# Attention and a routed expert layer on one core: most normalisers of the linear attention sent through memory instead of through TensorE, and turned tokens and logits in one product

## What is computed

```python
q, k, v = jnp.split(x @ W_qkv, 3, axis=-1)          # 16 heads of 64
q, k = relu(q @ W_f + b_f), relu(k @ W_f + b_f)
kv = einsum('bhnd,bhne->bhde', k, v)
out = einsum('bhnd,bhde->bhne', q, kv)
normalizer = einsum('bhnd,bhd->bhn', q, k.sum(axis=2))
out = out / (normalizer[..., None] + 1e-06)
x = layernorm(x + out @ W_out + b_out)
probs = softmax(x @ gate_w.T); topk_probs, topk_idx = top_k(probs, 2)
y = for each of the two: gelu(x @ w1[e] + b1[e]) @ w2[e] + b2[e]
x = layernorm(x + sum(y * topk_probs))
```

## Time and profile before

| | us |
|---|---|
| median of three runs | 456.76 |
| lowest and highest | 455.43, 457.03 |
| profiled execution | 455.49 |
| its span from first to last instruction | 453.7 |
| PE busy | 426.3 |
| DVE busy | 323.0 |
| ACT busy | 276.7 |
| POOL busy | 162.5 |
| mean granted TensorE clock | 0.983 of full speed |

### The profile page before, as it was taken

One profiled execution on the slowest core, in us unless ns is written; L12 is line 12 of the kernel. 1 busy time (PEld: TensorE's weight loads), 2 busy tenths in 40 slices (PEclk: granted clock), 3 DMA queues, 4 the chain that ended last, 5 costly groups with the idle time before them and its releaser, 6 DMA issues.

```text
span 453.7 us, 8859 instructions
## 1 busy us (share of the span) xinstructions
PE 426.3 (94%) x2784; PEld 340.6 (75%) x2784; DVE 323.0 (71%) x937; ACT 276.7 (61%) x554; POOL 162.5 (36%) x164
## 2 busy tenths in 40 slices
PE   7899999999999999999999999889999999999940
PEld 6777677677676676676776656479999999999940
DVE  3846968968968968968968998665774434456785
ACT  4755666666667666656756655349555655555565
POOL 3111002332331331431431421055777755555550
PEclk9999999999999999999999999999999999999985
DMA  8990210200200200200100060499696999498534
GB/s 215 315 217 3 75 65 0 95 24 2 94 25 0 95 24 1 94 26 1 72 24 1 25 241 16 143 344 304 173 242 219 284 380 311 134 362 311 180 114 139
DMA packets 40013, 61.16 MB, mean 135 GB/s; under 512 B 6287, under 2 KB 27284, under 8 KB 39840
## 3 DMA queue, kind: packets, MB, share of 16 engines
q1 hardware_dynamic: 30992, 50.00, 35.2%
q0 software_dynamic: 4544, 8.54, 5.4%
q10 hardware_dynamic: 4432, 2.07, 1.5%
HBM read 44.55 MB, written 17.49 MB: 137 GB/s over the span
## 4 chain that ended last, share of the span: by engine, by line
PE 85%; DVE 7%; DMA 3%; ACT 2%; issue 1%; ACTq 1%; POOL 0%; POOLq 0%; DVEq 0%; SPq 0%
PE psO L583 11%; PE psA L473 10%; PE psA L474 10%; PE psA L475 10%; PE psG L715 9%; PE psS L715 6%; PE psA L562 5%; PE psG L473 4%; PE psG L605 3%; PE psG L474 3%; PE psG L475 3%; PE psG L574 3%; PE psA L630 3%; DMA cst<-consts 2%; PE psS L519 1%
## 5 line engine op out<-in xcount | busy, mean ns | idle before, releaser
L433 POOL DMA_INDIRECT expert_rows<-rows,pos x64 | 62.0, 969 | 101.0 <-PE psA L475 65.1
L458 POOL DMA_INDIRECT expert_results<-q_act,kT x56 | 55.3, 988 | 36.7 <-DVE q_act L1237 26.4
L738 ACT ACTIVATE kT<-psA,bf_col 128x512 f32<-128x512 f32 x64 | 44.0, 688 | 34.8 <-PE psA L475 34.4
L583 PE MATMUL psO<-qn,mixed 128*128 128x512 f32 x128 | 64.2, 594 | 0.0
L738 ACT ACTIVATE q_act<-psA,bf_col 128x512 f32<-128x512 f32 x64 | 44.1, 689 | 26.1 <-PE psA L475 25.6
L904 DVE TENSOR_TENSOR k_lo<-psA,k_hi 128x512 fp32r<-128x512 f32 x64 | 43.9, 687 | 8.2 <-ACT k_hi L738 7.8
L715 PE MATMUL psG<-x_raw,q_act 128*128 x384 | 46.9, 275 | 0.2 <-ACT q_act L878 0.2
L1131 DVE TENSOR_TENSOR qn<-q_act,psG 128x512 f32<-128x512 f32 x64 | 42.9, 681 | 5.1 <-PE psG L574 5.0
L715 PEld LDWEIGHTS psG<-x_raw,q_act 128*128 128x128 f32 x384 | 44.9, 192 | 0.6 <-issue 0.6
L562 PEld LDWEIGHTS psA<-cst,kT 128*128 128x128 f32 x256 | 31.3, 140 | 16.0 <-issue 4.6
L738 ACT ACTIVATE k_hi<-psA 128x512 fp32r<-128x512 f32 x64 | 38.3, 598 | 7.3 <-PE psA L562 7.2
(11 more groups left out here) (202 smaller groups left out, 1045.5 us busy)
## 6 DMA issues: line engine op xcount, KB each, us to landing
k_hi<-expert_weights SPq DMA_DIRECT2D x15, 578.0 KB
k_lo<-expert_weights SPq DMA_DIRECT2D x15, 578.0 KB, 5.3
w_more<-expert_weights SPq DMA_DIRECT2D x9, 578.0 KB, 5.2
expert_weights<-w_more SPq DMA_DIRECT2D x8, 512.0 KB, 2.9
kT<-expert_rows SPq DMA_DIRECT2D x28, 132.0 KB, 4.7
w_raw<-w SPq DMA_DIRECT2D x8, 256.0 KB, 3.4
x_raw<-w SPq DMA_DIRECT2D x1, 2048.0 KB, 9.8
x<-expert_results SPq DMA_DIRECT2D x4, 512.0 KB, 5.8
```

Of the source, the lines that this page charges most:

```text
L433: pool.indirect_dma_start(xs, bass.IndirectOffsetOnAxis(ap=pos_2[o % 2][:, j, k:k + 1], axis=0), rows_2[o % 2][:, j, k, :], None).then_inc ...
L458: pool.indirect_dma_start(ys, bass.IndirectOffsetOnAxis(ap=xrow[r][:, c, D:D + 1].bitcast(I32), axis=0), yrow[u][:, c, :], None, bounds_ch ...
L583: mm(psO[:, :], mixed[:, c, :], qn[:, c % 4, :], start=c == 0, stop=c == CH - 1).then_inc(o_pe, 1)
L738: return act.activation(out_, in_, func, **kw)
```

## The change

1. `RELAYED = (3, 1, 1, 1, 1, 1, 1, 8)` gives for each batch p the first chunk whose normalisers don't go through PE. For these chunks SP, once both reciprocals are there, writes the two rows of `rn` eight times each to a memory tensor (7 writes, or 5 for batch 0), and then, chunk by chunk when its write has landed, reads them onto 128 partitions. The copies lie in a new buffer `bc` and in parts of `x_raw`, `xT_raw` and `gm` that are free then; the reads into `gm` wait for `mix`. `normalise(c)` waits for the read and takes its second operand from there.
2. The gate weights stand beside the identity in `turn_gate` [128 x 136], and one product per 128 tokens gives the turned tokens and their logits, three into `psO`, one into `psS`. `first_norm` now waits for the scaled logits, which are two instructions, and `ranks` for `first_norm`.
3. ACT makes the first half of the split norms ahead of the second gram copy, in batch 7 both halves.
4. The rows of block 0 are turned between the outputs of batch 7, and their low part stands ahead of `zT`. The last logits are scaled a step later, behind `xT_lo` of block 2.
5. Block 37 too releases its second layer in halves (`HALVED`).
6. The load of `w2_all` waits for normaliser 56, since copies lie in `x_raw`.

```diff
+RELAYED = (3, *(1 for _ in range(1, B - 1)), CH)
+COPIES = 8
+HALVED = NBLK - 2
+        rs = nc.dram_tensor("normalisers", [CH, 2, COPIES, S], F32, kind="Internal").ap()
-        gwc = sb("gwc", [P, E])
+        turn_gate = sb("turn_gate", [P, P + E])
+        bc = sb("bc", [P, 2, S])
+        def copies_at(c, p):
+            def tokens(q):
+                return x_raw[:, q * TILES:(q + 1) * TILES, :].rearrange("p t d -> p (t d)")
+            free = [bc[:, 0, :], bc[:, 1, :], tokens(p)]
+            if p:
+                free = free + [tokens(p - 1), xT_raw[:, (p - 1) * S:p * S]]
+            return (free + [gm[:, 0:S], gm[:, S:]])[c - RELAYED[p]]
...
+            for b in range(B):
+                for ex, _ in SPLIT_AT.get(b, ()):
+                    keep_split(ex)
+                if b < B - 1:
+                    sp.wait_ge(n_step, N_STEPS * (b + 1))
+                    for c in range(RELAYED[b], CH):
+                        row = c % 4 * QUAD + 2 * c
+                        sp.dma_start(rs[c], rn[row:row + 2, 1, None, :].broadcast_to([2, COPIES, S])).then_inc(r_out[c], 16)
+                    for c in range(RELAYED[b], CH):
+                        if c == CH - 2:
+                            sp.wait_ge(m_pe, 2 * (b + 1))
+                        sp.wait_ge(r_out[c], arrivals(c, b))
+                        sp.dma_start(copies_at(c, b), rs[c][:, :, None, :].broadcast_to([2, COPIES, DH // COPIES, S])).then_inc(bc_in[c], 16)
+            sp.wait_ge(qn_done, CH * (B - 1))
...
                 for j in range(TILES):
-                    last = mm(psS_l[:, j, :], zT[:, j * P:(j + 1) * P], gwc[:, :], start=True, stop=True)
-                last.then_inc(l_pe, 1)
-                for j in range(TILES):
-                    last = pe.transpose(psO_z[:, j, :], zT[:, j * P:(j + 1) * P], con("ident"))
+                    last = mm(z_at[j], zT[:, j * P:(j + 1) * P], turn_gate[:, :], start=True, stop=True)
                 last.then_inc(z_pe, 1)
...
-                    if prev and c + 1 < CH:
+                    if prev and c + 1 < RELAYED[p]:
                         spread_norm(c + 1)
...
+                    if b == B and c == CH - 1:
+                        turn_rows(0)
                     if prev and c:
                         output(c - 1)
...
+                    gram_copy(0)
+                    if prev:
+                        fill(p)
+                    act.wait_ge(r_l, b)
+                    norm_half(0)
+                    if b == B - 1:
+                        norm_half(1)
+                    gram_copy(1)
+                    if b < B - 1:
+                        norm_half(1)
...
-                    dve.wait_ge(bc_pe, CH * p + c + 1)
+                    relayed = c >= RELAYED[p]
+                    if relayed:
+                        dve.wait_ge(bc_in[c], arrivals(c, p))
+                    else:
+                        dve.wait_ge(bc_pe, sum(RELAYED[0:p]) + c + 1)
...
-                if n < NBLK:
-                    at = slice(n % 2 * BLK, (n % 2 + 1) * BLK)
...
+                if 1 <= n < NBLK:
+                    rows_low(n)
+                if n == 2:
+                    scale_logits(B - 1)
```

More of the change, by code:

```diff
@@ L198, in program @@
         endi = sb("endi", [1, E], I32)
-        past = [sb(f"past{i}", [1, LATE * len(ERAS) * E]) for i in range(2)]
+        past = [sb(f"past{i}", [1, EARLY * 2 * E]) for i in range(2)]
         tab = sb("tab", [1, 3, NBLK])
@@ L228, in program @@
         bankA = [psA[:, i // 2, i % 2 * 512:(i % 2 + 1) * 512] for i in range(4)]
-        psS_l = psS[:, 0:TILES * E].rearrange("p (t e) -> p t e", e=E)
-        psO_z = psO[:, :].rearrange("p (t d) -> p t d", d=D)
+        psO_l = psO[:, 0:(TILES - 1) * (D + E)].rearrange("p (t d) -> p t d", d=D + E)[:, :, D:]
+        z_at = [psO[:, j * (D + E):(j + 1) * (D + E)] for j in range(TILES - 1)] + [psS[:, (2 * TILES + 1) * E:(2 * TILES + 1) * E + D + E]]
         psS_c = psS[:, TILES * E:(2 * TILES + 1) * E].rearrange("p (t e) -> p t e", e=E)
@@ L234, in program, with arrivals @@
         psY2 = [bank[:, 0:2 * D].rearrange("p (t d) -> p t d", d=D) for bank in (psG[:, 1, :], psS)]
+        def copies_at(c, p):
[5 more added lines that the diff above has]
+            return (free + [gm[:, 0:S], gm[:, S:]])[c - RELAYED[p]]
+        def arrivals(c, p):
+            return 16 * sum(c >= RELAYED[q] for q in range(p + 1))
         def bank_of(n):
@@ L239, in result_at @@
         def result_at(n, t):
-            return psX2[bank_of(n)][:, 0:D] if n == NBLK - 1 and t else psY2[bank_of(n)][:, t, :]
+            return psX2[bank_of(n)][:, 0:D] if n >= HALVED and t else psY2[bank_of(n)][:, t, :]
         def before(n):
@@ L270, in program @@
         in_xr0, in_fold_q, in_fold_v, tab_step = (sem(n) for n in ("in_xr0", "in_fold_q", "in_fold_v", "tab_step"))
+        r_out, bc_in = ([sem(f"{n}{c}") for c in range(CH)] for n in ("r_out", "bc_in"))
         r_h, r_l, bc_pe, in_spread, spread_ready = (sem(n) for n in ("r_h", "r_l", "bc_pe", "in_spread", "spread_ready"))
@@ L337, in _, with keep_split @@
             load_w1(1)
-            for ex in range(E):
+            def keep_split(ex):
                 sp.wait_ge(w1_l, ex + 1)
@@ L672, in attention @@
                     mix(1)
-            for b in range(B + 1):
-                attention(b)
             def turn_rows(n):
@@ L715, in second_layer @@
                         last = mm(result_at(n, t), hT[v][:, c, t * P:(t + 1) * P], w2_all[:, ds(expert * (FC * D) + c * D, D)], start=c == 0, stop=c == FC - 1)
-                    if n == NBLK - 1 and t == 0:
+                    if n >= HALVED and t == 0:
                         last.then_inc(e_half, 1)
                 last.then_inc(e_down, 1)
+            for b in range(B + 1):
+                attention(b)
             for n in range(NBLK + 2):
-                if n < NBLK:
+                if 1 <= n < NBLK:
                     turn_rows(n)
@@ L837, in attention, with gram_copy @@
                         exponents(p)
-                    for h in range(2):
+                    def gram_copy(h):
                         act.wait_ge(g_pe, 2 * b + h + 1)
@@ L842, in attention, with norm_half @@
                         hi(gm[:, h * 512:(h + 1) * 512], psG[:, h, :]).then_inc(g_done, 1)
-                        if h == 0 and prev:
-                            fill(p)
-                    act.wait_ge(r_l, b)
-                    for h in range(2):
+                    def norm_half(h):
                         half = slice(h * S // 2, (h + 1) * S // 2)
@@ L971, in gone @@
             def gone(cum, n, k):
[L973 removed]
+                table_ = (past if n == EARLY else late_past)[0][:, 0:n * k].rearrange("p (n k) -> p n k", k=k)
                 tb(dve.tensor_tensor(table_, cum[:, None, 16:16 + k].broadcast_to([1, n, k]),
@@ L978, in summed @@
             def summed(to, by, n, k):
-                table_, scaled = (past[i][:, 0:n * k].rearrange("p (n k) -> p n k", k=k) for i in range(2))
+                table_, scaled = ((past if n == EARLY else late_past)[i][:, 0:n * k].rearrange("p (n k) -> p n k", k=k) for i in range(2))
                 tb(dve.tensor_tensor(scaled, table_, by[:, None, 0:k].broadcast_to([1, n, k]), ALU.mult))
```

59 lines of the change are left out of this document (33 added, 26 removed).

## The result

| us | before | this | |
|---|---|---|---|
| median | 456.31 | 488.91 | ratio 1.071, interval 1.068 to 1.074 |
| lowest and highest | 455.43, 457.03 | 487.35, 489.44 | four runs each |
| span of the profiled execution | 453.7 | 487.6 | +33.9 |
| mean granted TensorE clock | 0.983 | 0.943 | |

The account below looks back on a forecast made before the run. PE, busy 94% of the span, was taken as the bound. Terms of -1.2 + 1.2 + 2.6 + 3.0 + 0.4 = 6.0 us won took the median from 456.76 to 450.8, range 445.5 to 461.

Parts of the forecast that it names:

- L: Key part: time from second reciprocal's end (T0) until chunk 1's copies land; taken as 6.1 us, costing 1.2 in six batches.
- Writes go out every 0.38: SP's queue: seven relay writes issue 0.38 us apart, so 2.7 until the first read.
- The rule for turning L into time: Key part: break-even at L = 5.9; each us less wins one per batch until 4.2, each more costs one.
- Few engines: Rival, chance 0.35: two-partition writes carried by 2 of 16 DMA engines; L 6.3 to 7.7, run 452.0 to 460.4.
- Crowded engines: Rival, chance 0.15: first read shares DMA engines with six other reads and scatters; L = 8.0, run 462.2.
- Early: Rival, chance 0.12: chunk 1's read lands as the fetches do, L = 5.5 or less; run 447.6, at best 441.3.
- Batch 1 of the loop: Loop batch 1 relays only batch 0's chunks 3 to 7: no wait, five spread products gone, 1.2 us won.
- Batch 7 wins nothing and loses beyond 5.9: Loop batch 7, bound by DVE with its block table, gains nothing below L = 5.9 and loses beyond.
- Logits and turned tokens: Per batch four 136-column products replace small passes and transposes: 2.6 us won, bounds nothing to 6.1.
- End of the attention and tail: PE waits removed at the attention's end: 1.0, 1.1 and 0.9 won; block 37 stored in halves: 0.4 won.
- A spread product at 0.24: Each spread product takes 0.24 us of PE's time; 64 become 17.
- The later chunks are no question: Relayed chunks after the first land within 1 us of each other; DVE needs one every 2 us.

Follow-up runs that it names:

- e7: Changed kernel with the seven writes made without the eight copies, each chunk read in two halves; 476.84 on a slower chip, ratio 0.990 to the kernel before.
- e6: Changed kernel with only SP's order altered, writes and reads alternating so two writes precede the first read; 485.63 on a slower chip, ratio 1.007 to the kernel before.
- e3: Changed kernel with one write of all 128 partitions in place of seven, each chunk read in two halves; 453.50, ratio 0.994 to the kernel before.
- e1: Changed kernel without any relay, all 64 spread products on PE, every other part kept; 449.75, ratio 0.985 to the kernel before.
- e10: As e7, but each chunk read in one transfer whose source is two rows, in place of two half reads; 623.98, one execution.
- e2: Changed kernel with only chunks 4 to 7 relayed in batches 1 to 6, four writes and four reads; 444.00, ratio 0.971 to the kernel before.
- e2b: The kernel of e2 measured again on the chip of e8 and e9; 443.67, ratio 0.972 to the kernel before.
- e8: As e7 with writes without copies and half reads, but chunks 2 to 7 relayed in batches 1 to 6; 441.77, ratio 0.968 to the kernel before.
- e9: As e8, but chunks 3 to 7 relayed in batches 1 to 6; 442.99, ratio 0.970 to the kernel before.
- e4: As e1, with ACT's order, block 0's rows, last logits' scaling and block 37 put back, leaving only the logits product; 453.89, ratio 0.994 to the kernel before.
- e5: As e6 with writes and reads alternating, but chunks 2 to 7 relayed in batches 1 to 6; 472.29 on a slower chip, ratio 0.980 to the kernel before.

## Why the prediction was wrong

**The step that failed: L, the time until chunk 1's copies are there.** It had two terms, and both were taken from a row of another shape.

- *"Writes go out every 0.38."* That is the row of a plain store. A write with a repeated dimension takes 0.6 or more, 0.8 in the mean of seven (5.6 together), against 0.29 without (e7): 2.9 more before the first read can go.
- *"I take that: L = 6.1", with 3.4 for the read.* The read landed after 5.7 (5.3 in the median), 2.3 more than the sum had. With only two writes ahead it lands after 3.8 (e6), or 3.0 by halves (e3). By the arrivals, 14 engines had their share done 0.6 to 1.0 us later than the sum had the whole, and the two engines that also carry the writes needed 0.7 to 1.7 us more.

Together 11.3 for 6.1. These two are stretches of time one behind the other, and not two causes that add up: while SP issued slowly, the two engines were at work on the pieces, and 63 of the 112 moved between 116 and 120 us. Had the issue cost 0.38, 56 pieces of writes and 8 of the read on each of them, at 0.114 each 7.3 us, would have ended 8.6 after T0 at the earliest, since the first piece moved 1.3 after it (an estimate from those figures). No run tells how L splits between the two causes. What is shown is that the writes ahead made it (e6 changes nothing but their place), and that L is good again when pieces and repeated dimension go (e3, e7).

The rule for turning L into time was nearly right: the batch grew by 6.8 over e1. Beyond the break-even of 5.9 the sum would have said 5.3 for the measured starts (11.2 in the mean of six batches). Over the other 1.5 stands the lower clock behind the hole: 3.4 to 4.6 us of work at half speed are up to 1.7 to 2.3 lost in each batch, enough for it; no run has the hole without the lower clock. Six times 6.8 is 41, and with what the other parts won (7) and batch 0's five products (1) that is the 33 measured. The break-even was somewhat high: e7 starts 5.7 after T0 and is 0.4 a batch longer than e1, so it lies near 5.3.

**Few engines.** This rival had the mechanism, with the condition under which it holds and its mark in the profile, and a chance of 0.35. Its price was wrong twice: it took a piece at 0.071 to 0.094 where one took 0.114 (0.082 in e10), and it kept the issue at 0.38. So it ended at L = 7.7 and its time at 460.4, and the range at 461, on the mild side of something that had no row. The trace of before had no transfer from two partitions, so its upper end should have been open: 64 pieces at the slowest piece of the trace, 0.129 (for 2.7 KB), on top of the slow issue that a pattern with one dimension more may cost, gives 8.3 for the pieces alone, and the landing behind them.

**Crowded engines** was at most a small part: the share is 0.12 until the read's issue, but 0.65 and 0.92 while it is under way, and its first 14 arrivals are there 4.0 to 4.4 us after its issue, not far from the 3.8 of e6. The last two, which set L, follow the last write, and e6 moves the same bytes with a start at 6.4. **Early** fell with L.

**Batch 1 of the loop** (+1.2): right, 1.2 in the table of stretches. **Batch 7 wins nothing and loses beyond 5.9**: right. It takes 34.85 to 35.12 in e2, e2b, e8 and e9 against 34.92 in e1, and 40.76 in the change.

**Logits and turned tokens** (+2.6): 2.8 by e4. The upper bound beside it was added up wrongly: 1.28 less 0.49, times eight, is 6.3 and not 6.1. **End of the attention and tail** (3.0 + 0.4): 4.1, all three waits gone; the sum for these parts was 0.7 short, which is within the spread of the runs. Without the relay the forecast would have been 450.3, and e1 took 449.75.

**A spread product at 0.24**: right, 0.22 to 0.24 in each of the five batches that the prediction called bound by PE, in e2, e2b, e9 and e8. Only in the mean over all six it looks like 0.19, since loop batch 7 wins nothing.

**"The later chunks are no question"**: right in the change and in e2 (they land about 1 us apart), wrong as soon as writes and reads alternate (e5, e6).

## What to carry to other kernels

The shape of a small transfer can cost more than its bytes: two partitions as the slowest dimension put it on two of 16 engines, a repeated dimension doubles its issue (0.60 to 0.66 for 0.29), and whatever is queued behind it, however well spread itself, waits for those two. When a wait is moved to the head of an engine's queue, first ask how much later the first relayed item could be used; here moving the start from chunk 1 to chunk 4, which also takes three of seven writes away, turned 7% slower into 2.9% faster. And where a price has no row of its shape, leave the range open on that side, and add the clock that a hole costs afterwards.

## What the runs showed of the hardware that was not expected

- A write of two rows repeated eight times costs SP's queue 0.60 to 0.66, and two in the row of seven 1.07 and 1.10; without the repetition 0.29, for 256 KB from 128 partitions 0.32.
- A piece of 2 KB took 0.114 on one of two busy engines when it was written to memory, and 0.082 in e10's reads; rows of transfers over 16 engines gave 0.071 to 0.094 for it.
- After 6.0 to 6.8 us without work PE's granted clock was 0.50 for the first 3.4 to 4.6 us of work, and one chunk's work took 3.8 us where the next took 2.0: up to 1.7 to 2.3 us lost per hole on top of the hole.
- An issue on SP took 5.1 us in the median and up to 7.9 (e10) when the two engines that carry it were full: a backlog on a few engines stops the issuing engine too.
- The same kernel takes 456 on two chips and 482 on a third; by e5 against e2 the 25 us lie behind the last reciprocals, a stretch that is mostly the expert part. Why is open.
